# Layer 0 of a four-layer graph kernel: elu's end as one maximum on VectorE, its addition on GpSimd, and the normalisation a step on

## The reference

```python
h = jnp.maximum(_layernorm(x, axis=-1), 0.0)
# layer 0: attention over the neighbours, then a norm over batch and feature, then elu
h_prime = jnp.einsum('bij,bjo->bio', attention, Wh)
mean = h_prime.mean(axis=(0, 2), keepdims=True)
var = h_prime.var(axis=(0, 2), keepdims=True)
h_prime = gamma[None, :, None] * (h_prime - mean) * jax.lax.rsqrt(var + BN_EPS) + beta[None, :, None]
out = h_prime + h
x = x + jax.nn.elu(out)
# head of layer 1
h = jnp.maximum(_layernorm(x, axis=-1), 0.0)
```

## Time and profile before

| | us |
|---|---|
| median of 3 runs | 1559.11 |
| lowest, highest | 1558.41, 1561.33 |
| the profiled execution's own time | 1559.02 |
| its span, first to last instruction | 1557.2 |
| VectorE busy | 1252.0 |
| GpSimd busy | 1014.2 |

### The profile page before, as it was taken

The page is one execution under the profiler, slowest core; times in us unless marked ns, Lnnn a source line. Parts: engine busy times, 40 slices in busy tenths (PEclk is TensorE's granted clock), DMA queues, the critical chain, the costliest instruction groups (busy, mean ns, idle before and its releaser), DMA issues.

```text
span 1557.2 us, 15741 instructions
## 1 busy us (share of the span) xinstructions
PE 921.7 (59%) x4155; PEld 616.8 (40%) x4155; DVE 1252.0 (80%) x1592; ACT 791.9 (51%) x2666; POOL 1014.2 (65%) x965
## 2 busy tenths in 40 slices
PE   1137564761678676468788856567515546656581
PEld 0014332320456565357676622222205546642230
DVE  7889586996899999999999449989857996856461
ACT  2025444667165565355767824457683565652230
POOL 2132388621898897659898868877547875448881
PEclk9999886985799999879999987787757787878796
DMA  9951477421222231101120044523115633247665
GB/s 340 227 206 60 121 205 194 144 70 59 87 58 83 68 101 48 48 7 41 42 61 28 15 142 142 142 88 108 35 44 180 180 114 108 69 140 209 183 202 146
DMA packets 101571, 176.83 MB, mean 114 GB/s; under 512 B 47489, under 2 KB 56225, under 8 KB 99425
## 3 DMA queue, kind: packets, MB, share of 16 engines
q0 software_dynamic: 31472, 102.93, 22.7%
q1 hardware_dynamic: 67280, 72.13, 14.8%
q10 hardware_dynamic: 2720, 0.68, 0.2%
HBM read 145.78 MB, written 34.10 MB: 116 GB/s over the span
## 4 chain that ended last, share of the span: by engine, by line
DVE 53%; POOL 19%; issue 10%; ACT 6%; PE 6%; DMA 4%; DVEq 0%; POOLq 0%; ACTq 0%; SPq 0%
DVE big L1783 14%; DVE big L1775 11%; POOL big L693 10%; POOL big L720 5%; ACT big L993 3%; DVE big L1779 3%; DVE big L1724 2%; PE PS L1358 2%; DVE big L1667 2%; DVE big L1603 2%; DVE big L1729 1%; DMA big<-in_adj 1%; DVE big L1767 1%; PE PS L1339 1%; DVE stats L1700 1%
## 5 line engine op out<-in xcount | busy, mean ns | idle before, releaser
L993 ACT ACTIVATE big<-big 128x64 f32<-128x64 f32 x1496 | 371.1, 339 | 155.1 <-DVE big L1740 144.3
L720 POOL TENSOR_TENSOR big<-big 128x512 f32<-128x512 f32 x373 | 377.5, 1043 | 70.2 <-DVE big L1740 65.9
L1358 PE MATMUL PS<-ident,big 128*128 128x128 f32 x1740 | 246.0, 305 | 143.8 <-ACT big L1102 64.1
L1783 DVE TENSOR_REDUCE big<-big 128x32 f32<-128x2048 f32 (+4 forms) x126 | 297.6, 2362 | 4.3
L1358 PEld LDWEIGHTS PS<-ident,big 128*128 128x128 f32 x1740 | 226.9, 160 | 160.3 <-ACT big L1102 68.7
L1339 PE MATMUL PS<-big,ident 128*128 128x512 f32 x348 | 190.7, 707 | 119.8 <-ACT big L993 75.7
L693 POOL DMA_INDIRECT big<-tab,SI x142 | 179.2, 1262 | 75.5 <-issue 40.6
L1775 DVE TENSOR_TENSOR big<-big,PS 128x2048 f32<-128x2048 f32 (+4 forms) x84 | 198.5, 2363 | 18.2 <-PE PS L1370 15.3
L693 POOL DMA_INDIRECT big<-h_rows,SI x142 | 137.5, 969 | 51.2 <-issue 27.9
L1339 PEld LDWEIGHTS PS<-big,ident 128*128 128x128 f32 x348 | 76.3, 227 | 224.1 <-issue 201.7
L1355 PE MATMUL PS<-big,ident 128*128 128x512 f32 x174 | 113.5, 818 | 64.6 <-POOL big L720 64.6
(11 more groups left out here) (181 smaller groups left out, 1628.5 us busy)
## 6 DMA issues: line engine op xcount, KB each, us to landing
big<-in_adj SPq DMA_DIRECT2D x16, 1024.0 KB, 6.1
tab<-big SPq DMA_DIRECT2D x64, 132.0 KB, 1.8
big<-tab SPq DMA_DIRECT2D x32, 264.0 KB, 3.6
h_rows<-big SPq DMA_DIRECT2D x32, 256.0 KB, 2.0
big<-h_rows SPq DMA_DIRECT2D x32, 256.0 KB, 2.8
big<-in_x SPq DMA_DIRECT2D x16, 256.0 KB, 5.2
big<-xs SPq DMA_DIRECT2D x4, 1024.0 KB, 9.0
h_table<-big SPq DMA_DIRECT2D x16, 256.0 KB, 2.0
```

Source lines behind the costliest of these rows:

```text
L720: ins = pool.tensor_tensor(bd(wbuf[:, i % NWB, j, :]), bd(rows[:, k + j, :]), over_d(S[:, h, k + j, :], B), ALU.mult)
L993: ins = act.activation(to, row, ACT.Copy, scale=S[:, h, k + j, b:b + 1])
L1358: mm = pe.matmul(to[:, q * P:(q + 1) * P], wbuf[:, i % NWB, k, q * P:(q + 1) * P], ident[:, :], start=(first and q == 0), stop=(last and q ...
L1783: run(dve.tensor_reduce(scores(u, t)[:, h, k:k + n, :].rearrange("p k b -> p (k b)"), bd(prod[:, 0:n * E]), AX.X, ALU.add))
```

## The change

VectorE's L1818 goes. What is left of `elu_add` is one instruction, max(exp(min(y, 0)) - 1, y), written to `no` and told by a new semaphore `elu_made`. GpSimd's step m now begins with a wait for it and an addition of `no` to X for tile m-6, and tells `x_added`. Mean, centring, squares, row ends and stores follow one step later: the mean of tile m-6 on VectorE, behind a wait for `x_added`, the centring of tile m-7 on GpSimd, `norm(1, m-7)` on ScalarE, the store of tile m-8 on SyncE. The other layers are untouched.

```diff
--- before.py
+++ after.py
@@ -380,6 +380,7 @@
         bn_rooted = sem("bn_rooted")
         elu_in = sem("elu_in")
         elu_exped = sem("elu_exped")
+        elu_made = sem("elu_made")
         z_mean = sem("z_mean")
         z_centred = sem("z_centred")
         z_squared = sem("z_squared")
@@ -581,7 +582,7 @@
                         for m in range(NT + 10):
                             load_self(u, m + AHEAD)
                             if u == 0:
-                                store_h(1, m - 7)
+                                store_h(1, m - 8)
                             if u == 2:
                                 store_h(2, m - 7)
                             if u == 3:
@@ -778,7 +779,11 @@
                                 finish2(m)
                                 centre(2, m - 6)
                             if u == 0:
-                                centre(1, m - 6)
+                                t = m - 6
+                                if 0 <= t < NT:
+                                    pool.wait_ge(elu_made, t + 1)
+                                    pool.tensor_tensor(X[:, t, :], no[:, t % 4, :], X[:, t, :], ALU.add).then_inc(x_added, 1)
+                                centre(1, m - 7)
                             gather(u, m + AHEAD)
                             if u == 4:
                                 put_back(m - 3)
@@ -1023,7 +1028,7 @@
                     bn_root(m - 3)
                     bn_out(m - 4)
                     elu_exp(m - 5)
-                    norm(1, m - 6)
+                    norm(1, m - 7)
                     exp(0, m)
 
                 for m in range(-2, NT * HEADS + 10):
@@ -1815,10 +1820,8 @@
 
                     if 0 <= t < NT:
                         o = no[:, t % 4, :]
-                        run(dve.scalar_tensor_tensor(X[:, t, :], o, 0.0, X[:, t, :], ALU.max, ALU.add))
                         dve.wait_ge(elu_exped, t + 1)
-                        tell(dve.scalar_tensor_tensor(X[:, t, :], na[:, t % 2, :], -1.0, X[:, t, :], ALU.add, ALU.add),
-                             x_added, t + 1)
+                        tell(dve.scalar_tensor_tensor(o, na[:, t % 2, :], -1.0, o, ALU.add, ALU.max), elu_made, t + 1)
 
                 def finish2(m):
 
@@ -1848,7 +1851,9 @@
                     add_terms(0, m)
                     bn_scale(m - 3)
                     elu_add(m - 5)
-                    norm(1, m - 5)
+                    if 0 <= m - 6 < NT:
+                        dve.wait_ge(x_added, m - 6 + 1)
+                    norm(1, m - 6)
                     elu_low(m - 4)
                     bn_stats(m - 2)
```

## The result

| | before | changed |
|---|---|---|
| median of 6 runs, us | 1560.03 (1557.81 to 1561.40) | 1565.93 (1561.82 to 1568.10) |
| ratio, changed to before | 1 | 1.0039, 95% interval 1.0022 to 1.0055 |
| profiled execution, own time and span, us | 1559.02, 1557.2 | 1566.19, 1564.3 |

The change makes the kernel 5.9 us slower. The forecast was 1563.4 within 1559.6 to 1567.0. Direction and range held. The sum behind the forecast was less good: it had layer 0 4.3 us longer, and layer 0 is 8.6 us longer.

The account below looks back on a forecast made before the run. GpSimd's gathers were taken to bound the queue phase, and VectorE mostly what follows. Terms of +2.1 to step 11, -1.6 in 12 to 15, +0.6 in 16 to 19 and +3.2 drain gave +4.3; forecast 1563.4 us, range 1559.6 to 1567.0.

Parts of the forecast that it names:

- the drain: Layer 0's end, after the last exponential: four groups of ScalarE relus instead of three, +3.0, plus 0.2 for the last tile.
- the queue phase: Steps 0 to 7, where GpSimd's gathers set the pace: removing L1818 was to be worth nothing there.
- the wait for the exponential: Steps 14 to 19: the maximum must wait 0.17 to 0.72 us for ScalarE's exponential, which L1818 had not needed.
- The restart in step 7: After the gathers, the addition stands ahead of the centring, so VectorE starts again one instruction later: +1.1 us.
- The collisions: Steps 8 to 11: VectorE instructions stopped by GpSimd's wide ones, three more hits at the old rate, +3.9 us.
- The bound of +7.4: Upper bound of the collisions in steps 8 to 11: all eight wide GpSimd instructions hit at 1.4 us each.
- The mean's instruction: VectorE's small L1701, held by GpSimd's addition from step 12 on: 0.40 us instead of 0.17, +0.23 a step.
- Fewer collisions: Rival: no further hit or only one or two in steps 8 to 11, 1559.5 to 1562 us; chance 0.25.
- The count: Rival: instruction count decides, every step from 8 to 18 gains 0.72 us, sum -3.9, 1555.2 us; chance 0.10.
- The new chain: Rival: in steps 10 to 13 additions queue behind gathers, 5 us for one such step, 1568 us or more; chance 0.10.

Follow-up runs that it names:

- The kernel with the maximum first: Kernel before, but elu's maximum comes first and needs the exponential, then the addition to X, both on VectorE: layer 0 +2.85 us, ratio to before 1.0023.
- the one with half an elu: Kernel before without L1818, so max(y, 0) is never added to x, and no replacement: layer 0 4.6 us shorter, ratio to before 0.9954.
- The later step alone: Kernel before, elu unchanged, with mean, centring, squares, row ends and stores one step later: layer 0 +2.2 us, ratio to before 1.0011.

## Why the prediction was right, and where its sum was not

Direction and time came as forecast, and most of the mechanism did. Part by part, the sum had +2.1 us to the end of step 11, -1.6 in steps 12 to 15, +0.6 from there to the last minimum and +3.2 in the drain. Measured are +4.24, -0.49, +1.47 and +3.42.

**Where the gain went** was forecast step by step. L1818's 11.6 us are worth nothing in the queue phase; in steps 16 to 19 the wait for the exponential takes their place: it reads 0.21 and 0.28 in steps 14 and 15 (0.17 and 0.24 were forecast), 0.65 in each of steps 16 to 18 (0.61), 0.77 in step 19 (0.72), and 0.77 for the last tile, in the drain. The kernel with the maximum first shows that wait apart from all else, and the one with half an elu shows that the count doesn't decide.

**The restart in step 7** was to cost 1.1 and cost 0.90: counted from the first gather, the sum of squares begins at 69.50 us where it began at 68.60. Ahead of it now stands the mean's reduction, which waits 8.51 us for the addition, and the sum itself then waits 0.72 for the square, where it had waited 7.30:

```profile
252.85 1.27 POOL L785 TENSOR_TENSOR big<-big 128x512 f32<-128x512 f32 x1
254.07 1.04 POOL L705 TENSOR_TENSOR big<-big,stats 128x512 f32<-128x512 f32 x1
...
254.22 0.69 DVE L1705 TENSOR_REDUCE stats<-big 128x8 f32<-128x512 f32 x1 [8.51 <-POOL big L785]
255.88 0.69 DVE L1710 TENSOR_REDUCE stats<-big 128x8 f32<-128x512 f32 x1 [0.72 <-ACT big L959]
```

**The drain** was to cost 3.2 and cost 3.42. The later step alone gave 3.0.

**The collisions were mis-sized.** The sum had three more stops at the size of the old ones, +3.9. In the trace stand two more, and the three old ones have about doubled (3.9 us to 7.6), together +6.1. The step that failed is "At the same rate that is three more hits, +3.9". I counted wide instructions, as if each were met by itself. They stand back to back, and a VectorE instruction that begins ahead of the pair stays until both are through. A pair is one obstacle of 2.3 us, not two of 1. Where the second of the pair waits for the stopped instruction itself, as the centring for the mean, the obstacle is the first alone. The bound of +7.4 did hold. One reading behind this term was wrong: that each of the three old stops ends within 0.15 us of a centring's end holds for two. The weighing at 299.41 goes on to 303.65, and the centring beside it ended at 300.96; that it was held is read from its 4.24 us for 2.83 alone.

**The mean's instruction was mis-sized** for the same kind of reason: 0.62 us, not 0.40, from step 12 on. I took the centring's 1.04 us for the addition. The addition has two full inputs; the centring has one and the tile's eight means, each held for 64 elements. The page of before has a row of another layer that would have told, GpSimd's L727, which adds two full arrays and takes 1278 ns on average. I read past it. The timeline of before shows besides that a small second input doesn't make the time short by itself: L753, with one row of 64 numbers repeated eight times, takes 1.28 us.

```profile
L727 POOL TENSOR_TENSOR big<-big 128x512 f32<-128x512 f32 x64 | 81.8, 1278 | 58.8 <-ACT big L1055 58.1
```
```profile
397.87 1.28 POOL L753 TENSOR_TENSOR big<-big,rows 128x512 f32<-128x512 f32 x1
```

That is 0.22 us in each of eight steps, 1.8 us, which with +2.2 of collisions is nearly all of the 4.3 us by which layer 0 exceeds the sum.

Against that stand 1.5 us in this execution that no step of the sum contains, the earlier start above all. The change doesn't explain them: the first gather begins anywhere from 185.4 to 191.4 us in the kernels here, in code that none of the edits touches. That the forecast time lies as near to the measured one as it does (1563.4 and 1565.9) is in part luck: layer 0's own growth is twice that of the sum.

**The rivals.** Fewer collisions: there were more. The count: -4.6 us in a run of its own, and nothing of it left in the whole. The new chain: the mean's reduction waits for the addition in two places, 14.5 us in all, of 8.5 at most:

```profile
DVE stats L1705 <- POOL big L785: 14.5, 2, 8.5
```

These are the first two tiles, at 235.7 and 254.22 us, in steps 6 and 7, where the gathers set the pace and VectorE waited before as well. From step 8 on there is none. No gather more was held up ahead of step 12 than before, and the longest takes 5.09 us in both kernels.

## What to carry to other kernels

Before an instruction is taken off the busiest engine, look at what the next one waits for: if another engine's result is late, the removed one was the cover of that latency and its time comes back as a wait. Each tile of work that a change puts a step later is paid once, in full, at the end, by the engine that is last there (here 3.0 us). And wide work that is added to GpSimd was charged twice here, for its own time and for what VectorE can't do meanwhile, all the more where it stands back to back with other wide work: price such a row as one obstacle, with each operation's time from a row with the same kinds of input.

## What the runs showed of the hardware

- A wide `tensor_tensor` on GpSimd, 128x512 in f32, takes 1.27 us with two different full inputs and 1.04 with the same array twice. With a broadcast second input it depends on the pattern: 1.04 for eight numbers a partition, each held for 64 elements (the centring), 1.28 for a row of 64 numbers repeated eight times (L753).
- A VectorE `tensor_scalar`, or a `tensor_tensor` of arrays in SBUF, that meets GpSimd's wide work stands still until the last wide instruction in a row is through, however small it is: one number a partition took 2.70 us in place of 0.16, a product of 128x104 took 3.00. Both began in the gather ahead of the row. The reductions of 128x512 (0.69 us) show no such stop beside the same work, nor does a reciprocal of 128x8 (0.20 us).
- The other way round, a gather of 0.95 us that begins in a long VectorE product lasts until 0.8 us behind the product's end. Layer 0 has nine such gathers ahead of step 12, before and changed. One that begins almost with the product passes: in the kernel before a gather at 321.60, 0.04 us behind the product's start, took 0.96 us. In the changed kernel one at 302.95, 0.05 us behind it, was held and took 3.60. Here in the changed kernel, and the first of the two stands in the earlier trace rows too:

```profile
259.54 3.36 DVE L1772 TENSOR_TENSOR big<-big 128x3072 f32<-128x3072 f32 x1
260.32 3.40 POOL L694 DMA_INDIRECT big<-tab,SI  x1 [0.30 <-issue]
...
275.88 5.51 DVE L1772 TENSOR_TENSOR big<-big 128x5120 f32<-128x5120 f32 x1
277.13 5.09 POOL L694 DMA_INDIRECT big<-tab,SI  x1 [0.30 <-issue]
```
